# Layer 1's value columns multiplied from centred rows between the steps of a rank search, FFN's part added later over 256 inner rows; the gate norm's weights multiplied on GpSimd

## Chip, cores and metric

One core of a Trainium2 chip runs one program. The metric is the device time of one execution in microseconds (us). Before the change the median of 3 runs is 1879.77 us.

## What is computed

Two layers over 625 graph nodes with 1024 features. The part that matters here is the end of layer 0 and the start of layer 1, cut from the reference:

```python
x = x + gnn(xn, ...) * gate(...) + mix(xn)             # layer 0's graph and attention parts
# layer 0's FFN
h = _layernorm(x, ln_g, ln_b)
h = _qlinear(h, w1)          # int8 rows times ternary weights; 1024 -> 256
h = gelu(h)
x = x + _qlinear(h, w2)      # the same, 256 -> 1024
# layer 1
xn = _layernorm(x)
... xn @ W for W of 4096 columns: graph W, Wq, Wk, Wv
def _quant_act_int8(x):
    amax = jnp.quantile(jnp.abs(x), 1.0 - 0.005)
```

The quantile needs one number out of all 625 x 1024 (later 625 x 256) absolute values: the rank search finds it in steps, each of which counts the values over some thresholds and then narrows them.

## The kernel before

The nodes stand as T = 5 row tiles of P = 125. A dense product of 625 x 1024 rows with 512 columns is a "group": eight chunks of weights (128 inner rows by 512 columns) by five tiles, each in three matmuls (`three`: high by high, low by high, high by low part), 120 matmuls. One stream of chunks feeds all groups. SP loads a chunk into one of 4 stages (`w_stage`), ScalarE or GpSimd makes the high part (`w_hi`; `split_act`, or the first half of `split_chunk`), GpSimd or VectorE the low part (`w_lo`; `split_low`, `split_dve`), and 8 slots hold them. A slot is free again (`w_used`) when the last row tile of a group has used its chunk. A turned group (`dense_turned`) computes its product transposed, with 24 shorter matmuls a chunk.

All engines' queues are written out by hand in program order; nothing reorders them but what semaphores hold back. The order of the stretch in question:

1. Layer 0's gate: `proj_second` feeds the transposed rows (PE transposes, ScalarE copies `xt_hi`, VectorE subtracts `xt_lo`); then two gate groups, the first in two passes (rows 0 to 2, rows 3 and 4), the second row by row (`dense_pe_rows`).
2. Beside the second group, row by row on VectorE: `gate_evac` (z = nat * ps, x1 = x1 + z), `norm_var`, `candidates` (the largest 8 of each 256 absolute values), `norm_rows` (a Newton step for the root, then (x1 - mean) * lng, then * root + lnb into `nat`).
3. `find_rank` over those candidates: five rounds of seven thresholds (`pick_pe`, `sum_dve`), then three finer steps. VectorE and TensorE take turns. Then the rows are quantised (`round_part`, `clip_part`), multiplied by `w1q`, GELU, and `find_rank` again over 256 columns.
4. `down_pe`/`down_add` add the FFN into x1 tile by tile; `down_var`, `again_scale`, `again_norm`, `tile_turn`, `tile_high`, `tile_low` normalise and transpose each tile.
5. Layer 1's eight groups in the order `L1_ORDER = (6, 2, 4, 3, 5, 7, 0, 1)`; 6 is the first half of the value columns, 2 to 5 are turned. The first group is done tile by tile, between the transposes of step 4:

```python
for m in range(T):
    PE.wait_ge(S("x_low_a"), m + 1)
    PE.wait_ge(S("down_free"), 6 if m < 2 else 2 * T)
    dense_part(c0, g0, (m,), beside_again(m))
```

From the second group on GpSimd splits each chunk, high and low part.

## Time and profile before

| | |
|---|---|
| median of 3 runs | 1879.77 us (1879.57 to 1880.76) |
| profiled execution, first to last instruction | 1878.8 us |
| TensorE busy | 1794.9 us (96%) |
| VectorE busy | 1023.3 us (54%) |
| ScalarE busy | 478.5 us (25%) |
| GpSimd busy | 701.1 us (37%) |
| mean granted TensorE clock | 0.979 |

The profiled execution's own time is its span, 1878.8 us, and what lies around it; the runs shown have a median 1.0 us above that span. A busy TensorE is one with a matmul under way; the granted clock is 1.0 at 2.4 GHz and 0.5 at 1.2 GHz. A wait is given in brackets behind a row, with the engine and the tile that ended it.

### The profile page before, as it was taken

The numbers are of one execution on the slowest core, as the hardware profiler recorded it, in microseconds if no ns is written. First come the engines' busy times: TensorE is split into PE (matmuls) and PEld (weight loads), VectorE is DVE, ScalarE is ACT, GpSimd is POOL, SyncE is SP. The second block draws the span as 40 slices with busy tenths as digits, with TensorE's granted clock in tenths as the row PEclk, the third lists the DMA queues.
The fourth block names the chain that finished last, engine by engine and source line by source line (L and its number), as shares of the span: only waits on it lengthen the run. The fifth ranks groups of instructions, "written<-read, shape, count | busy, mean of one in ns | idle before, by whom it ended". The sixth has DMA issues, their size and how long they took to land.

```text
span 1878.8 us, 28666 instructions
## 1 busy us (share of the span) xinstructions
PE 1794.9 (96%) x9953; PEld 1477.4 (79%) x9953; DVE 1023.3 (54%) x2540; ACT 478.5 (25%) x1055; POOL 701.1 (37%) x609
## 2 busy tenths in 40 slices
PE   6999999999999999999999999954999999999999
PEld 4876689987777778787777887742899888878987
DVE  7888999997254543526354356786632224362311
ACT  3139956662010110101011145243100000111100
POOL 2110000003634435353534444200485552345862
PEclk9999999999999999999999999956999999999999
DMA  4532222224213121231313534110354351113322
GB/s 134 154 109 77 73 86 79 75 67 129 91 38 89 45 72 56 66 86 47 94 33 113 172 84 131 45 46 7 96 164 146 104 156 51 37 55 118 90 73 66
DMA packets 129282, 162.23 MB, mean 86 GB/s; under 512 B 14288, under 2 KB 75368, under 8 KB 128922
## 3 DMA queue, kind: packets, MB, share of 16 engines
q1 hardware_dynamic: 100848, 120.93, 21.5%
q10 hardware_dynamic: 22250, 23.53, 4.0%
q0 software_dynamic: 6080, 16.40, 2.9%
q8 instruction: 63, 1.03, 0.2%
q14 instruction: 41, 0.34, 0.1%
HBM read 135.51 MB, written 25.30 MB: 86 GB/s over the span
## 4 chain that ended last, share of the span: by engine, by line
PE 84%; DVE 6%; ACT 6%; issue 1%; DVEq 1%; DMA 1%; POOL 0%; ACTq 0%; SPq 0%
PE ps L367 22%; PE ps L368 22%; PE ps L369 21%; PE ps L1236 9%; PE ps L892 3%; ACT sc_col L838 2%; ACT sc_row L837 1%; PE ps L1201 1%; DVE w_lo L318 1%; PE ps L881 1%; PE ps L1156 1%; DMA nat<-in_x 1%; ACT w_hi L313 1%; PE ps L1183 1%; PE ps L1211 0%
## 5 line engine op out<-in xcount | busy, mean ns | idle before, releaser
L367 PE MATMUL ps<-w_hi,xt_hi 128*125 128x512 f32 x1320 | 539.0, 408 | 9.1 <-DVE xt_lo L549 3.5
L256 POOL TENSOR_TENSOR w_hi<-w_stage,zero 128x512 fp32r<-128x512 f32 x256 | 276.8, 1081 | 684.4 <-PE ps L369 670.0
L368 PE MATMUL ps<-w_lo,xt_hi 128*125 128x512 f32 x1320 | 523.0, 396 | 0.0
L369 PE MATMUL ps<-w_hi,xt_lo 128*125 128x512 f32 x1320 | 521.5, 395 | 0.0
L259 POOL TENSOR_TENSOR w_lo<-w_stage,w_hi 128x512 fp32r<-128x512 f32 x256 | 346.2, 1352 | 20.1
L367 PEld LDWEIGHTS ps<-w_hi,xt_hi 128*125 128x125 f32 x1320 | 246.6, 187 | 67.1 <-DVE xt_lo L549 4.3
L369 PEld LDWEIGHTS ps<-w_hi,xt_lo 128*125 128x125 f32 x1320 | 246.0, 186 | 63.3
L368 PEld LDWEIGHTS ps<-w_lo,xt_hi 128*125 128x125 f32 x1320 | 246.3, 187 | 53.5
L367 PE MATMUL ps<-xt_hi,w_hi 128*128 128x314 f32 x736 | 250.5, 340 | 1.3 <-DVE ring L2430 0.6
L369 PE MATMUL ps<-xt_hi,w_lo 128*128 128x314 f32 x736 | 225.9, 307 | 0.0
L368 PE MATMUL ps<-xt_lo,w_hi 128*128 128x314 f32 x736 | 225.7, 307 | 0.0
L367 PEld LDWEIGHTS ps<-xt_hi,w_hi 128*128 128x128 f32 x736 | 139.0, 189 | 6.8 <-POOL w_lo L259 1.1
L368 PEld LDWEIGHTS ps<-xt_lo,w_hi 128*128 128x128 f32 x736 | 139.5, 190 | 2.7
L369 PEld LDWEIGHTS ps<-xt_hi,w_lo 128*128 128x128 f32 x736 | 139.0, 189 | 0.0
L1420 DVE TENSOR_TENSOR nat<-nat,ps 125x512 f32<-125x512 f32 x80 | 53.9, 687 | 120.6 <-PE ps L369 120.2
L1286 ACT ACTIVATE xt_hi<-mtmp 128x313 fp32r<-128x313 f32 (+1 forms) x128 | 59.5, 465 | 194.1 <-DVEq L1390 194.1
L1236 PE MATMUL ps<-a_hi,xn_hi 125*128 125x313 f16 (+1 forms) x640 | 106.4, 297 | 1.7 <-DVE mtmp L1386 1.6
L1236 PE MATMUL ps<-a_hi,xn_lo 125*128 125x313 f16 (+1 forms) x640 | 106.3, 296 | 0.0
L313 ACT ACTIVATE w_hi<-w_stage 128x512 fp32r<-128x512 f32 x118 | 73.0, 629 | 108.1 <-PE ps L369 62.4
L856 DVE TENSOR_SCALAR hot_col<-iota,slot 128x626 f16<-128x626 f16 x240 | 91.6, 382 | 0.1
L292 POOL DMA_DIRECT2D pre<-ring x30 | 16.2, 540 | 194.7 <-DVE ring L476 192.8
L1236 PEld LDWEIGHTS ps<-a_hi,xn_hi 125*128 125x128 f16 x640 | 61.5, 97 | 26.9 <-issue 2.4
...
## 6 DMA issues: line engine op xcount, KB each, us to landing
...
```

The costliest lines, as they stand in the source:

```text
L256: POOL.tensor_tensor(w_hi[:, q, :], w_stage[:, q % NST, :], zero[:].to_broadcast([128, 512]), ALU.add).then_inc(S("hi_done"), 1)
L259: POOL.tensor_tensor(w_lo[:, q, :], w_stage[:, q % NST, :], w_hi[:, q, :].bitcast(F32), ALU.subtract).then_inc(S("split_done"), 1)
L313: ALE.activation(w_hi[:, c % NSL, :], w_stage[:, c % NST, :], ACT.Copy).then_inc(S("hi_done"), 1)
L367: PE.matmul(dst, l_hi, r_hi, start=first, stop=False)
L368: PE.matmul(dst, l_hi, r_lo, start=False, stop=False)
L369: return PE.matmul(dst, l_lo, r_hi, start=False, stop=last)
L838: ALE.activation(sc_col[j][:], sc_lo[j][:], ACT.Copy, scale=e_col1[:, bass.ds(c, 1)]).then_inc(S("sc_scaled"), 1)
L856: DVE.tensor_scalar(hot_col[q][:], iota1_16[:], slot[:, 0, bass.ds(c, 1)], None, ALU.is_equal)
L892: PE.matmul(group_banks(gm)[0], hot_row[q][:, 0:P], hot_col[q][:, 0:C1], start=(j == 0), stop=(j == 1), skip_group_check=True)
L1236: return PE.matmul(dst, x16[:, t, k * 128:(k + 1) * 128], a16[:, t, h0:h0 + hn], start=first, stop=last)
L1286: ALE.activation(xt_hi[:, j // 2, h0:h0 + hn], mtmp[j % 4][:, 0:hn], ACT.Copy).then_inc(S("mt_hi"), 1)
L1420: DVE.tensor_tensor(u_, u_, ps[0:P, m, :], ALU.add).then_inc(S("bank_free"), 1)
```

## The change

- Layer 1's group of value columns 6 comes second in `L1_ORDER`, and is computed in two parts. With c the gate's result less its row mean, the normalised row is (c + f - mean of f) * root, f being the FFN's output. c @ W is computed beforehand: 120 matmuls from `xc_hi`, `xc_lo`, the transposed centred rows, stored to DRAM in `p_part`. f's part goes over its 256 inner rows: `w2k` is the ternary second FFN weight less its mean over the columns, w2k @ W is 32 matmuls stored in `m_part`, and `late_pe` later multiplies the quantised inner rows with that in 20 matmuls; `evac_late` adds `p_late` and the bias.
- These 152 matmuls (`part_pe`) are given out by `in_gap(n)`, n at a time, between the steps of the rank searches, in the first FFN product and in the norm that follows. Their eight chunks are a group of their own (`C_GAP`).
- `w2k` is made on VectorE (the mean) and ScalarE (the subtraction), transposed by 16 transposes on TensorE in the gate's second pass, and copied by ScalarE.
- Rows 0 to 3 of the gate norm: ScalarE subtracts the mean (`centre`), GpSimd multiplies with `lng` (`times_gain`); VectorE's Newton step and last multiplication for row m stand after row m+1's gate work. The centred rows stay in x1; ScalarE adds the mean back after the norm of step 4.
- GpSimd also makes the low parts of the `C_GAP` chunks, subtracts `xc_lo` (`low_x`), and splits all eight chunks of layer 1's first group.
- The first dense group of layer 1 is a turned one, and starts when all five tiles are done.

The diff, cut to its core:

```diff
+    C_REL, C_PROJ, C_GATE, C_GAP, C_L1, D_L1 = 80, 208, 224, 240, 248, 240
+    L1_ORDER = (2, 6, 4, 3, 5, 7, 0, 1)
+    TURNED1 = (0, 2, 3, 4)
+    LATE = 1
...
+    def turn_w2(i):
+
+        PE.wait_ge(S("w2_centred"), 2)
+        if i == 3:
+            PE.wait_ge(S("w2_copied"), 1)
+        for k in (2 * i, 2 * i + 1):
+            for j in range(FFN0 // 128):
+                o = (k % 2) * FFN0 + j * 128
+                t_ = PE.transpose(ps[:, W2_BANKS[i], o:o + 128], w2k[:, j, k * 128:(k + 1) * 128], ident[:])
+        t_.then_inc(S("w2_turned"), 1)
...
+    def beside_gate(k):
+        if k in (3, 4, 5, 7):
+            turn_w2((3, 4, 5, 7).index(k))
...
+    def low_x(m):
+
+        POOL.wait_ge(S("x_hi"), T + m + 1)
+        POOL.tensor_tensor(xc_lo[:, m].rearrange("p k n -> p (k n)"), xc_raw[:, m].rearrange("p k n -> p (k n)"),
+                           xc_hi[m][:].rearrange("p k n -> p (k n)").bitcast(F32), ALU.subtract).then_inc(S("x_low"), 1)
+
...
+    def part_pe():
+
+        PE.wait_ge(S("bank_free"), (g1 + 2) * T + 4)
...
+        for m in range(T):
+            PE.wait_ge(S("x_low"), T + m + 1)
+            PE.wait_ge(S("part_out"), m + 1)
+            dst = ps[0:P, PART_BANKS[m % 2], :]
+            for k in range(KT):
+                PE.matmul(dst, xc_hi[m][:, k, :], w_hi[:, k, :], start=(k == 0), stop=False)
+                yield
+                PE.matmul(dst, xc_hi[m][:, k, :], w_lo[:, k, :], start=False, stop=False)
+                yield
+                t_ = PE.matmul(dst, xc_lo[:, m, k, :], w_hi[:, k, :], start=False, stop=(k == KT - 1))
+                if m == T - 1:
+                    t_.then_inc(S("w_used"), 1)
+                elif k == KT - 1:
+                    t_.then_inc(S("part_full"), 1)
+                if k == KT - 1:
+                    part_out(2 + m, p_part[m], P)
+                yield
...
+    for c in range(C_GATE + KT, C_GATE + KT + 2):
+        split_act(c)
+    for j in range(FFN0 // 128):
+        ALE.wait_ge(S("w2_room"), 1)
+        ALE.activation(w2k[:, j, :], w2q[:, j, :], ACT.Identity, bias=w2_mean[:, j:j + 1]).then_inc(S("w2_centred"), 1)
+    for i in range(4):
+        copy_w2(i)
+    for c in range(C_GATE + KT + 2, C_GAP):
         split_act(c)
...
+        if k == 5:
+            DVE.wait_ge(S("wq_done"), 2)
+            DVE.tensor_reduce(w2_mean[:], w2q[:], AX.X, ALU.add)
+            DVE.drain()
+            DVE.tensor_scalar(w2_mean[:], w2_mean[:], -1.0 / D, None, ALU.mult).then_inc(S("w2_room"), 1)
...
+    def times_gain(m):
+
+        POOL.wait_ge(S("x_norm"), T + m + 1)
+        POOL.tensor_tensor(nat[:, m, :], x1[:, m, :], lng[:], ALU.mult).then_inc(S("h_gain"), 1)
...
+            DVE.drain()
+            DVE.wait_ge(S("h_gain"), m + 1)
             DVE.scalar_tensor_tensor(o, o, r, lnb[:], ALU.mult, ALU.add).then_inc(S("h_norm"), 1)
 
     rk_up = small("rk_up", [P, 4, 7], F16)
...
         gate_evac(1, m)
         norm_var(m)
+        square_act(m)
+        if m < T - 1:
+            centre(m)
         if m >= 1:
-            candidates(habs, "h_abs", D, m - 1)
-        norm_rows(m)
-        square_act(m)
-        if m == T - 1:
-            copy_h(0)
-            copy_h(1)
-        absolute(nat, habs, "h_abs", D, m)
+            norm_root(m - 1)
+            norm_out(m - 1)
+            absolute(nat, habs, "h_abs", D, m - 1)
+        if m >= 2:
+            candidates(habs, "h_abs", D, m - 2)
+        for c in {2: (0, 1), 3: (2, 3, 4), 4: (5, 6, 7)}.get(m, ()):
...
+    for m in range(3):
+        times_gain(m)
+    for c in range(3):
+        split_low(C_GAP + c, c)
+    times_gain(3)
+    for c in range(3, KT):
+        split_low(C_GAP + c, c)
+    for m in range(T):
+        low_x(m)
+
+    turn_x(0)
+    turn_h(0)
+    in_gap(32)
+    turn_x(1)
+    copy_x(1)
+
+    done["chunks"] += 5 * KT
...
@@ -1723,15 +1882,14 @@
                     t_ = PE.matmul(ps[0:n_, 0, j:j + 1], hot[:, j, o:o + n_], ones_b[0:P, :], start=(o == 0), stop=(o == 128),
                                    skip_group_check=True)
             t_.then_inc(S("rk_part"), 1)
+            in_gap(2)
             PE.wait_ge(S("rk_copied"), i + 1)
             PE.matmul(ps[:, 1, 0:columns], ones16[:], q_part7[:, 0:columns], start=True, stop=True).then_inc(S("rk_count"), 1)
...
+    def turn_rest(i):
+
+        if i in (0, 2, 4):
+            turn_h(1 + i // 2)
+            copy_h(1 + i // 2)
+        elif i < ROUNDS + 1:
+            turn_x(2 + i // 2)
+            copy_x(2 + i // 2)
...
+    in_gap(8)
+    down_pe(0)
+    in_gap(8)
...
+    DVE.tensor_scalar(h_mean[:], h_neg[:], -1.0, None, ALU.mult)
+    mk = sig(DVE.drain(), "dve_step")
+    DVE.wait_ge(S("w_used"), NSL + C_GAP + KT)
+    DVE.tensor_copy(gq_whole[:], gq_t[:]).then_inc(S("gq_whole"), 1)
+    wait(ALE, mk)
+    for m in range(T):
+        mk_mean = sig(ALE.activation(x1[:, m, :], x1[:, m, :], ACT.Identity, bias=h_mean[:, m:m + 1]), "act_step")
+
+    for c in range(C_L1, C_L1 + NSL):
+        split_chunk(c, c % NSL, c // NST + 1)
...
+    in_gap(6)
+    for m in range(1, T):
+        if m + 2 < T:
+            down_pe(m + 2)
+        tile_turn(m, AGAIN)
+        in_gap(12)
+    in_gap(8 * KT * T)
+    PE.wait_ge(S("x_low"), AGAIN + T)
+    PE.wait_ge(S("part_out"), 2 + T)
+
+    def late_pe(g):
+
+        PE.wait_ge(S("gq_whole"), 1)
+        for m in range(T):
+            PE.wait_ge(S("bank_free"), (g + g0) * T + (3, 3, 4, 5, 5)[m])
+            for k in range(FFN0 // 128):
+                if m == 0:
+                    PE.wait_ge(S("split_done"), NST + c0 + g * KT + k + 1)
...
+                if m == T - 1:
+                    last.then_inc(S("w_used"), 1 if k == 0 else KT - 1)
+                elif k == FFN0 // 128 - 1:
+                    last.then_inc(S("bank_full"), 1)
+
```

The first place where the order of a queue differs: ScalarE (ACT), from the last of the gate's fed chunks to the splitting of the second gate group's eight chunks (`w_hi<-w_stage`; the first of the rows shown is the first group's last). Before:

```order
L313 ACTIVATE w_hi<-w_stage 128x512 [waits w_used,landed3]
L313 ACTIVATE w_hi<-w_stage 128x512 [waits w_used,landed0]
L313 ACTIVATE w_hi<-w_stage 128x512 [waits w_used,landed1]
L313 ACTIVATE w_hi<-w_stage 128x512 [waits w_used,landed2]
L313 ACTIVATE w_hi<-w_stage 128x512 [waits w_used,landed3]
```

Now:

```order
L312 ACTIVATE w_hi<-w_stage 128x512 [waits w_used,landed3]
L312 ACTIVATE w_hi<-w_stage 128x512 [waits w_used,landed0]
L312 ACTIVATE w_hi<-w_stage 128x512 [waits w_used,landed1]
L1619 ACTIVATE w2k<-w2q,w_mean 128x1024 [waits w2_room] x2
L1478 ACTIVATE w2k_t<-ps 128x512 [waits w2_turned,w2_room]
L1478 ACTIVATE w2k_t<-ps 128x512 [waits w2_turned] x3
L312 ACTIVATE w_hi<-w_stage 128x512 [waits w_used,landed2]
L312 ACTIVATE w_hi<-w_stage 128x512 [waits w_used,landed3]
```

Six of the second gate group's eight chunks now stand behind the four copies of `w2k_t`, the last of which waits for transposes that TensorE does after chunk 7 of the first gate group's second pass.

The second place: GpSimd (POOL), from the low parts of the projection and gate chunks (x24) on. Before it waits there for VectorE's low parts, and then runs its loop over layer 1's chunks:

```order
L276 TENSOR_TENSOR w_lo<-w_stage,w_hi 128x512 [waits hi_done] x24
L264 UNCONDITIONAL_BRANCH [waits split_done]
L264 ISA
L255 ISA [waits landed0]
L256 TENSOR_TENSOR w_hi<-w_stage,zero 128x512 [waits w_used]
```

Now:

```order
L279 TENSOR_TENSOR w_lo<-w_stage,w_hi 128x512 [waits hi_done] x24
L1762 TENSOR_TENSOR nat<-x_8789,lng 125x1024 [waits x_norm] x3
L279 TENSOR_TENSOR w_lo<-w_stage,w_hi 128x512 [waits hi_done] x3
L1762 TENSOR_TENSOR nat<-x_8789,lng 125x1024 [waits x_norm]
L279 TENSOR_TENSOR w_lo<-w_stage,w_hi 128x512 [waits hi_done] x5
L1544 TENSOR_TENSOR xc_lo<-xc_raw,xc_hi_12097 128x1000 [waits x_hi]
L1544 TENSOR_TENSOR xc_lo<-xc_raw,xc_hi_12098 128x1000 [waits x_hi]
L1544 TENSOR_TENSOR xc_lo<-xc_raw,xc_hi_12099 128x1000 [waits x_hi]
L1544 TENSOR_TENSOR xc_lo<-xc_raw,xc_hi_12100 128x1000 [waits x_hi]
L1544 TENSOR_TENSOR xc_lo<-xc_raw,xc_hi_12101 128x1000 [waits x_hi]
L259 TENSOR_TENSOR w_hi<-w_stage,zero 128x512 [waits w_used,landed0]
L262 TENSOR_TENSOR w_lo<-w_stage,w_hi 128x512 [waits hi_done]
```

GpSimd's 17 operations between the gate and layer 1 are new, and so is its splitting of the first group's chunks; the fourth multiplication with `lng` stands behind three low parts.

The third place: ScalarE at the end of the norm of step 4 (`xt_hi` of the last tile is the last that it does for it). Before:

```order
L2094 ACTIVATE xt_hi<-ps 128x4x125 [waits x_turn]
L2262 DMA bias_o<-in_bias 125x1024
L2264 DMA a_bd<-in_pm 64x64
L2265 DMA a_bd<-in_pm 64x64
L2383 DMA pre<-ring 125x512 [waits bank_free] x5
```

Now:

```order
L2261 ACTIVATE xt_hi<-ps 128x4x125 [waits x_turn]
L2466 ACTIVATE x_8789<-x_8789,h_mean 125x1024 [waits dve_step]
L2466 ACTIVATE x_8789<-x_8789,h_mean 125x1024 x4
L2482 DMA bias_o<-in_bias 125x1024
L2484 DMA a_bd<-in_pm 64x64
L2485 DMA a_bd<-in_pm 64x64
L1555 ACTIVATE part<-ps 125x512 [waits part_st0,w_used]
L1557 DMA p_part<-part 125x512 [waits part_out]
```

The copy that empties the last bank of the part products (`part<-ps`) stands behind five additions of the mean and three DMAs; TensorE's first matmul of the first dense group of layer 1 waits for it:

```order
L366 MATMUL ps<-xt_hi,w_hi 128x314 [waits split_done,bank_free,part_out,x_low]
```

## Rows read from the trace of the kernel before

**Rows 1.** The page: the chain that ended last, shares of the span by engine.

```profile
PE 84%; DVE 6%; ACT 6%; issue 1%; DVEq 1%; DMA 1%; POOL 0%; ACTq 0%; SPq 0%
```

**Rows 2.** Windows: length, busy PE, PEld, DVE, ACT, POOL (xinstructions), PEclk, DMA, GB/s.

```profile
1236.00:1240.00 4.00, 3.14 (x22) 2.87 (x23) 3.74 (x19) 3.02 (x6) 0.00 (x0) 0.50 0.06 23
...
1308.00:1312.00 4.00, 3.11 (x8) 2.43 (x9) 3.53 (x8) 1.52 (x2) 0.00 (x0) 0.50 0.00 0
```

**Rows 3.** Groups, TensorE, 1166.4 to 1222.5: the gate's matmuls, high by high.

```profile
L367 PE MATMUL ps<-w_hi,xt_hi 128*125 128x512 f32 x80 | 31.6, 395 | 1.8 <-DVE xt_lo L1169 1.8
```

**Rows 4.** Timeline of the gate's feed: start, duration, engine, operation, [idle before].

```profile
1160.30 0.68 DVE L1168 TENSOR_TENSOR xt_lo<-ps,xt_hi 128x500 fp32r<-128x500 f32 x1 [1.01 <-ACT xt_hi L1163]
...
1161.38 0.70 PE L1156 MATMUL ps<-ident,nat 125*128 125x125 f32 x5
...
1166.47 0.50 PE L367 MATMUL ps<-w_hi,xt_hi 128*125 128x512 f32 x1 [1.75 <-DVE xt_lo L1169]
```

**Rows 5.** Timeline, VectorE: two reductions of different length in the rank search.

```profile
1257.18 0.28 DVE L1823 TENSOR_REDUCE q_cnt<-q_hot 125x31 f16<-125x124 f32 x1
...
1259.77 0.42 DVE L1823 TENSOR_REDUCE q_cnt<-q_hot 125x63 f16<-125x252 f32 x1
```

**Rows 6.** Timeline: four low parts on GpSimd, and VectorE beside them.

```profile
1191.13 5.78 POOL L276 TENSOR_TENSOR w_lo<-w_stage,w_hi 128x512 fp32r<-128x512 f32 x4
...
1194.56 1.20 DVE L1580 SCALAR_TENSOR_TENSOR x<-x,z 125x512 f32<-125x512 f32 x1
```

**Rows 7.** Timeline, VectorE (ScalarE in the first), gate rows 1 to 4.

```profile
1208.49 1.15 ACT L1627 ACTIVATE habs<-x,h_neg 125x1024 f32<-125x1024 f32 x1 [0.50 <-DVEq L1621]
...
1213.59 0.68 DVE L1572 TENSOR_TENSOR z<-nat,ps 125x512 f32<-125x512 f32 x1
1214.30 0.69 DVE L1580 SCALAR_TENSOR_TENSOR x<-x,z 125x512 f32<-125x512 f32 x1
...
1215.40 1.41 DVE L1599 MAX8 cand<-habs 125x8 f32<-125x256 f32 x4
...
1217.89 1.28 DVE L1645 SCALAR_TENSOR_TENSOR nat<-x,h_neg,lng 125x1024 f32<-125x1024 f32 x1
...
1227.30 0.68 DVE L1572 TENSOR_TENSOR z<-nat,ps 125x512 f32<-125x512 f32 x1
...
1234.41 1.41 DVE L1599 MAX8 cand<-habs 125x8 f32<-125x256 f32 x4
```

**Rows 8.** Timeline of the last norm: a step beside GpSimd's splitting, and without it.

```profile
1661.44 1.49 POOL L256 TENSOR_TENSOR w_hi<-w_stage,zero 128x512 fp32r<-128x512 f32 x1
1663.01 1.28 POOL L259 TENSOR_TENSOR w_lo<-w_stage,w_hi 128x512 fp32r<-128x512 f32 x1
...
1662.18 0.77 DVE L532 SCALAR_TENSOR_TENSOR t<-rs,va 125x1 f32<-125x1 f32 x1
...
1685.99 0.22 DVE L532 SCALAR_TENSOR_TENSOR t<-rs,va 125x1 f32<-125x1 f32 x1
```

**Rows 9.** Timeline, VectorE: the seven thresholds of a round of the rank search.

```profile
1246.61 1.29 DVE L1762 TENSOR_SCALAR r_hot<-r_hi,q_took 125x160 bf16<-125x160 int16 x7
```

**Rows 10.** Timeline, the norm before layer 1, and the start of its first two groups.

```profile
1297.28 1.40 DVE L2040 SCALAR_TENSOR_TENSOR x<-ps,qrs,x 125x512 f32<-125x512 f32 x2
...
1308.15 1.26 DVE L2101 TENSOR_TENSOR xt_lo<-ps,xt_hi 128x500 fp32r<-128x500 f32 x2
1308.89 0.79 PE L367 MATMUL ps<-w_hi,xt_hi 128*125 128x512 f32 x1 [3.44 <-DVE xt_lo L2101]
...
1313.85 0.16 DVE L530 RECIPROCAL rs<-t 125x1 f32<-125x1 f32 x1 [1.01 <-ACT t L2082]
...
1315.13 1.26 DVE L2101 TENSOR_TENSOR xt_lo<-ps,xt_hi 128x500 fp32r<-128x500 f32 x2
...
1334.14 0.60 ACTq L2265 DMA_DIRECT2D a_bd<-in_pm  x1
...
1343.59 0.38 PE L367 MATMUL ps<-xt_hi,w_hi 128*128 128x314 f32 x1 [0.65 <-DVE ring L2430]
```

More of the change, by code:

```diff
@@ new lines, in part_out @@
+    def part_out(n, dst, rows):
+        if n < 1 + T:
+            ALE.wait_ge(S("part_full"), n + 1)
+        else:
+            ALE.wait_ge(S("w_used"), NSL + C_GAP + KT)
+        if n >= 2:
+            ALE.wait_ge(S(f"part_st{n % 2}"), 16 * (n // 2))
+        ALE.activation(part[0:rows, n % 2, :], ps[0:rows, PART_BANKS[n % 2], :], ACT.Copy).then_inc(S("part_out"), 1)
+        ALE.wait_ge(S("part_out"), n + 1)
+        ALE.dma_start(dst, part[0:rows, n % 2, :]).then_inc(S(f"part_st{n % 2}"), 16)
@@ L1490, in build, with in_gap @@
+    steps_left = part_pe()
+    def in_gap(n):
+        for _ in itertools.islice(steps_left, n):
+            pass
     MAGIC = 1.5 * 2.0 ** 23
@@ L1644, in norm_rows, with norm_out @@
         DVE.tensor_tensor(r, r, t, ALU.mult)
-        DVE.scalar_tensor_tensor(o, x1[:, m, :], h_neg[:, m:m + 1], lng[:], ALU.add, ALU.mult)
-        DVE.drain()
+    def norm_out(m):
+        r, o = rs[:, m:m + 1], nat[:, m, :]
         if m == T - 1:
+            DVE.scalar_tensor_tensor(o, x1[:, m, :], h_neg[:, m:m + 1], lng[:], ALU.add, ALU.mult)
+            DVE.drain()
             c = slice(0, 512)
@@ L2127, in build @@
     clip_part(gq_t[:, :, (T - 1) * P:NODES], KT + T)
-    for m in range(4):
+    in_gap(8)
+    down_pe(0)
+    in_gap(8)
+    for m in range(1, 3):
         down_pe(m)
```

389 lines of the change are left out of this document (238 added, 151 removed).

## The prediction

> **What bounds the kernel now.** The chain of waits puts 84% of the span on TensorE, 6% each on VectorE and ScalarE [rows 1], so only stretches where TensorE waits can give or cost much. I read the windows and the groups next, to find those, then the timelines of each. There are three. In the gate TensorE needs 240 matmuls (80 of each kind) for the 56 us of the view [rows 3]: 0.233 us each, 5.6 for a row tile's 24. VectorE needs more in the second group: its work on a row begins every 6.86 us (1213.59 for row 2, 1227.30 for row 4) [rows 7]. In the rank searches the two take turns; the granted clock is 0.50 [rows 2]. In the norm before layer 1 VectorE's cadence is 1315.13 - 1308.15 = 7.0 us a tile, of which 1.0 is a wait for ScalarE [rows 10], against 5.6 of matmuls. So the group of value columns, 28 us on TensorE, already lies almost wholly under VectorE's norm. Moving it away frees little there; what VectorE, ScalarE and GpSimd do in its place decides. That is the main point of this forecast.
>
> **The change part by part.** The profiled execution lasted 1878.8 us, 1.0 under the median of the runs; I sum against 1878.8. Times after T0 count from `down_add(0)`, 1297.28 [rows 10].
>
> (a) The mean of `w2k` in the feed: reducing 252 elements takes 0.14 us more than 124 [rows 5], so 2048 cost 2.2 us on VectorE. Its steps there wait 1.0 for ScalarE each [rows 4], which hides about one. Ends 0 and 2.2; I take **+1.0**.
>
> (b) Sixteen transposes in the gate's second pass, 0.14 each (5 in 0.70) [rows 4], 2.2 in all, with a stop of 0.1 for ScalarE's subtraction: **+2.3**. Nothing hides them, TensorE is busy in that pass.
>
> (c) The queue of the second gate group's chunks. ScalarE splits two, then subtracts the mean, then copies four banks, the last transposed behind chunk 7 of the pass; only then come chunks 2 to 7 (the first place shown). GpSimd's low parts take 5.78/4 = 1.45 each [rows 6]. So the group's first chunk finds its operands about 2.8 us after the pass's end and the last at 10.0; TensorE finishes row 0 10.7 us after the pass instead of 5.6: **+5.1**. Before, all eight were split ahead.
>
> (d) The gate rows. Before: row 0's work begins 4 x 6.86 before 1227.30, at 1199.9, and the last `candidates` end at 1235.8: 35.9 us [rows 7]. With the multiplication by `lng` (1.28) [rows 7] gone from rows 0 to 3, VectorE needs about 5.6 and keeps pace with TensorE: row 4 starts 22.3 after row 0. But its tail is longer: the 8.5 us of before (1227.30 to 1235.8), and now also row 3's last multiplication (1.3), two more `candidates` (1.4 each), and a wait of 2.4 for GpSimd's `times_gain(3)`, which stands behind three low parts; 0.3 of it overlaps: 14.7. That makes 37.0, +1.1.
>
> To this comes what GpSimd does to VectorE. In the last norm one and the same step of the root takes 0.77 beside GpSimd's splitting and 0.22 without it; the 0.77 end at 1662.95, which is where GpSimd's operation ends (1661.44 + 1.49) [rows 8]. In the gate x1 = x1 + z took 1.20 beside low parts, 0.69 without [rows 6, 7]. So the two shut each other out for a whole operation when VectorE reads two operands from SBUF. The new GpSimd operations are four multiplications of 1024 columns (2 x 1.28 [rows 8] = 2.6 us) and eight low parts of 1.45; VectorE's `gate_evac`, variance, root and last multiplication meet them. Laid out row by row (each `times_gain` starts 4.5 after a row's work begins), rows 1 to 3 run late by 0.6, 1.5 and 1.3, row 4 begins at 26.7, the wait for `times_gain(3)` ends at 31.8, row 3 is out at 35.0, row 4's root at 39.8 after two stops, its norm ends at 44.0 and the last `candidates` at 46.9. That is 9.9 more than 37.0. Ends 0 and 12 x 1.45 = 17; I take 9.9, **+11.0** with the above.
>
> The Trainium skill says the same of the ports (page SBUF — State Buffer, section "Who interferes with whom"): VectorE's second pair is shared with GpSimd, and whoever comes first holds it for the whole instruction. It adds that copies and `tensor_scalar` can take both pairs. By the page's rule the thresholds of the rank search would be shut out too; no row of this case has one beside GpSimd.
>
> (e) The first search. `in_gap(2)` fits into the 1.29 us of thresholds [rows 9]; the 32 matmuls ahead, the 5 in each finer step and TensorE's extra transposes of centred rows leave +0.8, after VectorE's own low parts (off its queue now) are taken off. GpSimd's five `low_x` of 2.6 stand beside it; a block costs at most 2.6 less the 1.0 that VectorE waits anyway, so 0 to 8.0 in all. VectorE's operations are about half of the two-operand kind: 4.2, together **+5.0**.
>
> (f) The up product and second search: matmuls in the gaps keep the clock up, which was 0.50 [rows 2]: **-0.7**. Ends -3 and +3.
>
> (g) The norm. VectorE's chain shortens to 6.1 a tile (the wait of 1.0 goes, since no dense matmuls hold the transposes) [rows 10], so the last low part would end at T0 + 31.3. But GpSimd splits layer 1's first eight chunks there, 1.49 and 1.28 [rows 8], in place of ScalarE and VectorE earlier; the blocks cost 0 to 12, and I take 7.7 by the 0.55 of rows 8 on some 14 steps: T0 + 39.0. Then ScalarE: the last `part<-ps` copy stands behind five additions of the mean (1.15 each [rows 7]) and three DMA issues (0.60 each [rows 10]), and TensorE waits for it (the third place shown). 5.8 + 1.8 + 0.6 = 8.1. The turned group starts at T0 + 47.2, where it started at 1343.59, T0 + 46.3 [rows 10]. It runs its first us at the low clock, as the first group did (8 matmuls in 3.11 us, 0.39 each [rows 2]): 1.5. Later `late_pe`, 20 x 0.233 = 4.7, and 2.2 of waiting, because GpSimd can split group 3's first chunks only when `late_pe` has freed slots. **+9.3**.
>
> Sum: 1.0 + 2.3 + 5.1 + 11.0 + 5.0 - 0.7 + 9.3 = +33.0; 1911.8 in the span, **1912.8** as a median.
>
> **The rivals.**
>
> R1, no blocking: the few long cases of rows 6 and 8 are not typical, and new operations fall between VectorE's. Then 9.9 + 4.2 + 7.7 = 21.8 go: 1891.0. For it: nearly all VectorE steps beside GpSimd in the trace are short enough to slip in. Against it: the match to the hundredth in rows 8. 0.19.
>
> R2, ScalarE's tail is hidden (another wait ends later, or the mean is added beside VectorE's last tile): -8.1, 1904.7. Against: the addition waits for a drain behind the last low part. 0.10.
>
> R3, other side: GpSimd is quick enough never to be waited for. That is 21.8, the 2.4 of `times_gain(3)`, the 5.1 of (c) and the 2.2 of (g), 31.5: 1881.3, not slower than before. It decides from about 0.7 us for 512 columns, which is VectorE's time for them [rows 7]. The rows show GpSimd at 1.28 to 1.49. 0.11, since all ends of (e) and (f) may add to it.
>
> R4, the clock stays at 0.50 through both searches, as it does now [rows 2]: some 60 matmuls in the first at 0.39 instead of 0.23, 8 us of it exposed, and 3 in the second: 1923.8. 0.08.
>
> R5, the thresholds are shut out too: (e) costs 0.8 + 8.0, +3.8, 1916.6. It is the port rule of the page named in (d). Nothing in the trace speaks for or against it. 0.05.
>
> That the change does not do what it says: 128 of the 152 matmuls stand ahead of the norm in program order, the rest in it. If chunks or `xc_lo` come late, TensorE stops in a gap, and that is in (e) and R4.
>
> **How the numbers follow.** The forecast has 0.47, R1 0.19, R2 0.10, R3 0.11, R4 0.08, R5 0.05. Some 0.2% (3.8 us) is what a measurement of this kernel can tell from no change. Not slower needs at most 1883.5: R3 mostly, with R1's lower edge (its (f) at -3). R3 I split 0.04 faster, 0.05 same, 0.02 slower, and give 0.02 of R1 to the two. So faster 0.05, same 0.06, slower 0.89. The range reaches from under R1 (1887, its (a) and (f) low) to 1923, which leaves out most of R3, half of R4 and the ends of (d) and (g), 0.18 in all. All of the forecast's own case lies in 1904 to 1921.
>
> **What the profile of after would show.** (b, c) A wait of TensorE of 2 to 3 us for `split_done` at the second gate group, and `w_hi` of its chunks 2 to 7 behind `w2k_t`. (d) From row 0's `gate_evac` to the last `candidates` some 47 us, 2.6 us for `nat` on GpSimd, VectorE steps of 0.2 that take 1 to 2, and VectorE's idle time ended by POOL in row 4. (e) Thresholds still 1.29, a search of 30 us rather than 26. (g) The last `xt_lo` 39 us after `down_add(0)`, the turned group 8 later, its wait ended by ACT `part`. The prediction is wrong if VectorE's steps keep their times beside GpSimd (R1), if TensorE's wait ahead of the turned group ends with `xt_lo` (R2), or if the feed or the searches wait for operands that I have as ready. A gain would need GpSimd's rows near 0.7.

## The result and the profile after

The changed kernel takes 1917.71 us (median of 4 runs, 1916.51 to 1919.33), beside 1880.26 for the one before on the same chip: a ratio of 1.0201, 95% interval 1.0189 to 1.0214. It is 37.5 us slower; whether that is more or less than 2% the interval leaves open. The forecast was 1912.8 with a range of 1887 to 1923: the result lies inside, 4.9 us above the forecast. The profiled execution spans 1915.2 us, 36.4 more than before; the sum of the prediction was 33.0.

To see where the 36.4 arise I divided both traces at six instructions, each a row of VectorE's or TensorE's timeline: the first `z<-nat,ps` of gate row 0, the copy `r_hi<-cand` that begins the first search, the first `h_t<-h_t,qs` behind it, `down_add(0)` (the first `x<-ps,qrs,x`, T0), the first matmul of the first turned group, and the last turned evacuation `ring_t<-ps,bias_t`.

| stage (us) | before | after | difference | forecast |
|---|---|---|---|---|
| start to row 0 (a, b, c) | 1200.1 | 1207.1 | +7.0 | +8.4 |
| gate rows (d) | 35.9 | 45.1 | +9.2 | +11.0 |
| first search (e) | 26.2 | 35.5 | +9.3 | +5.0 |
| up product, second search (f) | 35.1 | 37.4 | +2.3 | -0.7 |
| T0 to the first turned group (g) | 46.3 | 44.4 | -1.9 | +0.9 |
| from there to the last turned evacuation (g) | 125.2 | 135.8 | +10.5 | +8.4 |

The six differences make 36.4: behind the last of these points both kernels need 410.0 us.

The dividing points of the changed kernel in VectorE's timeline, and the steps read below (start, duration, operation, [idle before]); the rows of before at the same places are [rows 7, 10]:

```profile
1207.09 0.69 DVE L1692 TENSOR_TENSOR z<-nat,ps 125x512 f32<-125x512 f32 x1 [8.37 <-PE ps L368]
...
1231.40 0.67 DVE L1692 TENSOR_TENSOR z<-nat,ps 125x512 f32<-125x512 f32 x1
1232.10 1.68 DVE L1700 SCALAR_TENSOR_TENSOR x<-x,z 125x512 f32<-125x512 f32 x1
...
1234.48 1.56 DVE L1771 SCALAR_TENSOR_TENSOR t<-rs,va 125x1 f32<-125x1 f32 x1
...
1246.57 2.81 DVE L1786 SCALAR_TENSOR_TENSOR nat<-nat,rs,lnb 125x512 f32<-125x512 f32 x1
...
1252.14 0.24 DVE L1914 COPY r_hi<-cand 125x160 int16<-125x160 int16 x1
...
1256.23 2.16 DVE L1940 SCALAR_TENSOR_TENSOR q_took<-q_cand,q_took 128x1 f32<-128x1 f32 x1
...
1287.68 1.00 DVE L2153 TENSOR_SCALAR h_t<-h_t,qs 128x625 f32<-128x625 f32 x2
...
1325.05 1.40 DVE L2207 SCALAR_TENSOR_TENSOR x<-ps,qrs,x 125x512 f32<-125x512 f32 x2
```

Beside them GpSimd, in the changed kernel's timeline:

```profile
1233.19 2.84 POOL L1762 TENSOR_TENSOR nat<-x,lng 125x1024 f32<-125x1024 f32 x1
1235.98 2.53 POOL L279 TENSOR_TENSOR w_lo<-w_stage,w_hi 128x512 fp32r<-128x512 f32 x2
...
1246.06 2.77 POOL L1544 TENSOR_TENSOR xc_lo<-xc_raw,xc_hi 128x1000 fp32r<-128x1000 f32 x1
1256.07 2.30 POOL L1544 TENSOR_TENSOR xc_lo<-xc_raw,xc_hi 128x1000 fp32r<-128x1000 f32 x1 [7.24 <-ACT xc_raw L1538]
```

Three steps of VectorE end with an operation of GpSimd or right behind it. The step on one element that begins at 1234.48 ends at 1236.04, GpSimd's multiplication with `lng` at 1236.03. The addition of `lnb` that begins at 1246.57 has some 0.7 us of work and takes 2.81: GpSimd's subtraction holds it till 1248.83, and it ends 0.55 later. `q_took` from 1256.23 ends at 1258.39, `xc_lo` at 1258.37. That is the pattern of [rows 8], at the places forecast under (d) and (e).

TensorE in one round of the first search (4.46 us from one count to the next), and two windows of the same stretch (columns as in [rows 2]). First the timeline:

```profile
1263.23 1.73 PE L1882 MATMUL ps<-ones_b,r_hot 125*128 125x1 bf16 x14
1264.88 0.79 PE L1579 MATMUL ps<-w_lo,xc_hi 128*125 128x512 f32 x1
1265.47 0.63 PE L1581 MATMUL ps<-w_hi,xc_lo 128*125 128x512 f32 x1
1265.90 0.23 PE L1887 MATMUL ps<-q_part,ones 128*128 128x7 f16 x1
1265.99 1.91 PE L1528 MATMUL ps<-ident,x 125*128 125x125 f32 x8
1267.69 1.73 PE L1882 MATMUL ps<-ones_b,r_hot 125*128 125x1 bf16 x14
```

And the windows:

```profile
1252.00:1260.00 8.00, 6.81 (x44) 5.44 (x44) 5.56 (x23) 6.03 (x13) 2.30 (x1) 0.61 0.17 66
1260.00:1268.00 8.00, 8.00 (x44) 6.31 (x43) 4.01 (x22) 1.24 (x4) 2.31 (x1) 0.50 0.01 2
```

In the second window TensorE is busy for 8.00 of 8 us and the granted clock is 0.50, its lower level. VectorE is busy for half of it. In this search TensorE no longer takes turns with VectorE, it sets the length of the rounds. The prediction did not have that.

The gate's feed, the last step of it. Before, TensorE's five transposes stand together and it waits once, 1.75 us (TensorE's timeline of the kernel before, and [rows 4]):

```profile
1164.02 0.70 PE L1156 MATMUL ps<-ident,nat 125*128 125x125 f32 x5
```

In the changed kernel it waits twice, since VectorE is making the mean of `w2k`; and the last step of that, on two elements, starts beside a low part of GpSimd and ends with it, at 1164.00 and 1163.98:

```profile
1162.64 0.59 PE L1155 MATMUL ps<-ident,nat 125*128 125x125 f32 x4
1162.71 1.27 POOL L279 TENSOR_TENSOR w_lo<-w_stage,w_hi 128x512 fp32r<-128x512 f32 x1 [1.02 <-ACT w_hi L312]
1162.80 1.20 DVE L1674 TENSOR_SCALAR w_mean<-w_mean 128x2 f32<-128x2 f32 x1
1164.83 0.33 PE L1155 MATMUL ps<-ident,nat 125*128 125x125 f32 x1 [1.59 <-DVE xt_lo L1168]
1166.90 0.50 PE L366 MATMUL ps<-w_hi,xt_hi 128*125 128x512 f32 x1 [1.75 <-DVE xt_lo L1168]
```

The wait at the second gate group and the two ends of (g), from TensorE's timeline of the changed kernel:

```profile
1199.89 0.50 PE L366 MATMUL ps<-w_hi,xt_hi 128*125 128x512 f32 x1 [1.44 <-POOL w_lo L279]
...
1201.13 0.50 PE L366 MATMUL ps<-w_hi,xt_hi 128*125 128x512 f32 x1 [0.28 <-POOL w_lo L279]
...
1369.40 0.60 PE L366 MATMUL ps<-xt_hi,w_hi 128*128 128x314 f32 x1 [7.36 <-issue]
...
1406.24 0.41 PE L366 MATMUL ps<-xt_hi,w_hi 128*128 128x314 f32 x1 [2.38 <-POOL w_lo L262]
```

TensorE's last matmul ahead of 1369.40 are transposes that end at 1362.0. What it waits for is not named there ("issue"); VectorE's and ScalarE's rows show it:

```profile
1362.70 0.68 DVE L2268 TENSOR_TENSOR xt_lo<-ps,xt_hi 128x500 fp32r<-128x500 f32 x1 [0.15 <-ACT xt_hi L2261]
...
1364.57 4.25 ACT L2466 ACTIVATE x<-x,h_mean 125x1024 f32<-125x1024 f32 x4
1368.73 0.57 ACT L1555 ACTIVATE part<-ps 125x512 f32<-125x512 f32 x1
```

The last low part is done at 1363.38, T0 + 38.3 (forecast 39.0); `part` at 1369.30, and TensorE starts 0.1 us later.

### The profile page after: what moved, and what is told of

It is laid out like the page before. It is cut to its first block, busy times and chain, and to the rows that moved or that the text cites. A ratio compares the mean times of both kernels' runs of the same rounds, so it can differ in the third digit from the quotient of the medians.

```text
span 1915.2 us, 28990 instructions
## 1 busy us (share of the span) xinstructions
PE 1831.9 (96%) x10061; PEld 1499.7 (78%) x10061; DVE 1040.4 (54%) x2539; ACT 507.9 (27%) x1098; POOL 741.3 (39%) x630
## 4 chain that ended last, share of the span: by engine, by line
PE 85%; DVE 6%; ACT 5%; issue 2%; DVEq 1%; DMA 1%; POOL 1%; ACTq 0%; SPq 0%; POOLq 0%
PE ps L366 22%; PE ps L367 21%; PE ps L368 21%; PE ps L1235 9%; PE ps L891 3%; ACT sc_col L837 2%; ACT sc_row L836 1%; PE ps L1200 1%; DVE w_lo L317 1%; PE ps L880 1%; PE ps L1155 1%; DMA nat<-in_x 1%; PE ps L1182 1%; ACT w_hi L312 1%; PE ps L1210 0%
## 5 line engine op out<-in xcount | busy, mean ns | idle before, releaser
L366 PE MATMUL ps<-w_hi,xt_hi 128*125 128x512 f32 x1280 | 522.8, 408 | 8.5 <-DVE xt_lo L548 3.5
L367 PE MATMUL ps<-w_lo,xt_hi 128*125 128x512 f32 x1280 | 506.6, 396 | 0.0
L368 PE MATMUL ps<-w_hi,xt_lo 128*125 128x512 f32 x1280 | 505.3, 395 | 0.0
L262 POOL TENSOR_TENSOR w_lo<-w_stage,w_hi 128x512 fp32r<-128x512 f32 x258 | 349.6, 1355 | 20.2
L366 PEld LDWEIGHTS ps<-w_hi,xt_hi 128*125 128x125 f32 x1280 | 238.8, 187 | 66.2 <-POOL w_lo L279 5.5
L368 PEld LDWEIGHTS ps<-w_hi,xt_lo 128*125 128x125 f32 x1280 | 238.2, 186 | 61.3
L367 PEld LDWEIGHTS ps<-w_lo,xt_hi 128*125 128x125 f32 x1280 | 238.6, 186 | 51.5
L279 POOL TENSOR_TENSOR w_lo<-w_stage,w_hi 128x512 fp32r<-128x512 f32 x40 | 58.3, 1476 | 64.9 <-ACT w_hi L312 64.8
```

The costliest lines, as they stand in the source:

```text
L262: POOL.tensor_tensor(w_lo[:, q, :], w_stage[:, q % NST, :], w_hi[:, q, :].bitcast(F32), ALU.subtract).then_inc(S("split_done"), 1)
L279: POOL.tensor_tensor(w_lo[:, q, :], w_stage[:, q % NST, :], w_hi[:, q, :].bitcast(F32), ALU.subtract).then_inc(S("split_done"), 1)
L366: PE.matmul(dst, l_hi, r_hi, start=first, stop=False)
L367: PE.matmul(dst, l_hi, r_lo, start=False, stop=False)
L368: return PE.matmul(dst, l_lo, r_hi, start=False, stop=last)
```

## The experiments

Twelve kernels, all edits of the changed one. They ran on three chips, each beside the kernel before, whose median on these chips is 1880.0 to 1880.5. e1, e6, e7, e9 and e11 leave work out; the others keep all of it. "Less" and "more" below are against the changed kernel's 1917.71. The stages are cut as above.

| run | median | row 0 | gate | search | f | to turned | rest |
|---|---|---|---|---|---|---|---|
| after | 1917.71 | 1207.1 | 45.1 | 35.5 | 37.4 | 44.4 | 135.8 |
| e1_no_low_x | 1913.36 | 1207.2 | 43.0 | 34.1 | 37.3 | 44.3 | 135.8 |
| e2_rounds | 1920.59 | 1210.6 | 45.1 | 33.5 | 39.5 | 47.1 | 135.2 |
| e3_tail | 1911.93 | 1209.3 | 45.0 | 35.4 | 35.9 | 39.2 | 135.6 |
| e4_queue | 1913.37 | 1203.2 | 45.0 | 35.4 | 36.0 | 43.9 | 135.7 |
| e5_gain_dve | 1916.50 | 1208.2 | 45.3 | 35.4 | 37.6 | 44.5 | 136.0 |
| e6_no_gpsimd_low | 1908.46 | 1211.1 | 36.8 | 32.7 | 36.1 | 45.3 | 135.2 |
| e7_no_norm_split | 1909.99 | 1210.6 | 45.1 | 35.4 | 36.0 | 37.9 | 135.3 |
| e8_all | 1909.41 | 1206.2 | 45.0 | 33.5 | 38.7 | 41.2 | 135.8 |
| e9_no_turn_x | 1921.46 | 1210.5 | 45.0 | 37.3 | 37.3 | 44.3 | 135.8 |
| e10_tail_queue | 1907.50 | 1203.7 | 45.0 | 35.3 | 36.9 | 39.2 | 135.7 |
| e11_floor | 1890.52 | 1203.8 | 36.8 | 33.5 | 37.0 | 31.9 | 135.9 |
| e12_dve_low | 1906.29 | 1205.9 | 42.3 | 35.8 | 35.9 | 39.2 | 135.6 |

Two columns move without an edit to them, from one execution to the next. Row 0 comes up to 4 us later, partly because all that stands ahead of the gate's feed ends sooner or later, partly by the granted clock in the feed (the last section), and (f) lies between 35.9 and 37.6. So the stage that was edited decides what an edit did. A difference of two medians contains the rest too.

**e1_no_low_x.** GpSimd's five subtractions go.

```diff
-            t_ = ALE.activation(xc_raw[:, m, 4 * j:4 * j + 4, :], view, ACT.Copy)
+            t_ = ALE.activation(xc_lo[:, m, 4 * j:4 * j + 4, :], view, ACT.Copy)
-        POOL.tensor_tensor(xc_lo[:, m]..., xc_raw[:, m]..., xc_hi[m]..., ALU.subtract).then_inc(S("x_low"), 1)
+        POOL.sem_inc(S("x_low"), 1)
```

> The five subtractions that make xc_lo on GpSimd are left out (ScalarE's second copy writes the unsplit values into xc_lo, so the low parts are not low parts). Theory A, shutting out: in the changed kernel one-element steps of the rank search took 2.16, 0.48 and 1.41 us instead of 0.16 beside these subtractions, 3.6 us together, and the last gate row's additions of lnb took 1.60 and 2.81 instead of about 0.7, part of it beside the first of them. So the time falls by 4 to 6 us, and the steps go back to 0.16. Theory B, the first search is long because TensorE has more to do in each round (two matmuls ahead of the sum, eight transposes behind it): it falls by less than 1 us, and rounds of 4.1 us stay.

4.4 us less as a median, 3.5 in the stages: 2.1 in the gate, 1.4 in the search. A is right that they hold VectorE. But the search loses 1.4 where the held steps sum to 3.6, and the rounds keep 4.47 us: TensorE's own work covers the rest. B is right about the rounds that stay, and wrong about the sum.

**e2_rounds.** The two matmuls leave the rounds.

```diff
-            in_gap(2)
...
     down_pe(0)
-    in_gap(8)
+    in_gap(20)
```

> The two part matmuls in each of six rounds of the first search are moved behind the first product of the second FFN weight. Theory B: VectorE's wait between the cast of the counts and their comparison goes from 1.01 back to 0.28 us, 0.73 times 6 rounds = 4.4 us; the 12 matmuls cost about 1.4 where they go, so the time falls by 3. Theory A (only the shutting out makes the first search long): no change, or 1 us more.

The sign is wrong, 2.9 us more. The search does lose 2.0. But (f) grows by 2.1 and the norm by 2.7, and both stages can be read. VectorE's timeline of this run, behind `down_add(0)`:

```profile
1328.69 1.40 DVE L2206 SCALAR_TENSOR_TENSOR x<-ps,qrs,x 125x512 f32<-125x512 f32 x2
...
1333.10 1.41 DVE L2206 SCALAR_TENSOR_TENSOR x<-ps,qrs,x 125x512 f32<-125x512 f32 x2 [1.11 <-PE ps L2197]
```

`down_add(1)` waits for TensorE's second product, which stands behind 20 matmuls instead of 8. It starts 4.4 us behind the first, where it was 3.4 in the changed kernel (1325.05 and 1328.46). In (f) VectorE waits 6.40 us for GELU's first value instead of 4.10. ScalarE's timeline of this run shows why:

```profile
1300.69 0.60 ACT L1555 ACTIVATE part<-ps 125x512 f32<-125x512 f32 x1 [4.78 <-PE ps L1581]
...
1301.65 0.47 ACT L2181 ACTIVATE gl<-ps,qrs 125x256 f32<-125x256 f32 x1 [0.37 <-ACT part L1555]
```

With 12 part matmuls fewer ahead, the last matmul of a row tile of the part products now falls behind the up product, and the copy of that tile stands ahead of GELU in ScalarE's queue. GELU waits for a matmul that it does not need. In the changed kernel this copy is made ahead of the up product (1284.92), and in e8, which has the same move, it stands ahead of GELU again and waits 3.77 us. Moved out of a busy stage, the work became exposed in two others.

**e3_tail.** ScalarE's five additions and three DMAs move behind `in_gap(8 * KT * T)`.

```diff
-    wait(ALE, mk)
-    for m in range(T):
-        mk_mean = sig(ALE.activation(x1[:, m, :], ..., bias=h_mean[:, m:m + 1]), "act_step")
...
     in_gap(8 * KT * T)
+    wait(ALE, mk)
+    for m in range(T):
+        mk_mean = sig(ALE.activation(x1[:, m, :], ..., bias=h_mean[:, m:m + 1]), "act_step")
```

> ScalarE's five additions of the mean and its three DMAs move behind the last copy of the part products. Theory: TensorE waits for that copy alone, so the first turned group starts right behind the last xt_lo (1363.4 in the changed kernel, where it started at 1369.4): the time falls by 5.5 us. Rival: something else is as late (VectorE's work on c_nat till 1368.9, GpSimd's splitting, the late group's data), and it falls by less than 2.

5.8 us less, as expected, 5.2 of it in the stage of the edit. TensorE now starts behind the last low part (timeline of this run):

```profile
1364.18 0.68 DVE L2268 TENSOR_TENSOR xt_lo<-ps,xt_hi 128x500 fp32r<-128x500 f32 x1 [0.15 <-ACT xt_hi L2261]
...
1364.91 0.63 PE L366 MATMUL ps<-xt_hi,w_hi 128*128 128x314 f32 x1 [1.39 <-DVE xt_lo L2268]
```

**e4_queue.** Splits and copies take turns on ScalarE.

```diff
-    for i in range(4):
-        copy_w2(i)
-    for c in range(C_GATE + KT + 2, C_GAP):
-        split_act(c)
+    split_act(C_GATE + KT + 2)
+    for c, i in ((3, 0), (4, 1), (5, 2), (6, None), (7, 3)):
+        if i is not None:
+            copy_w2(i)
+        split_act(C_GATE + KT + c)
```

> ScalarE splits the second gate group's chunks 2 to 7 between the copies of w2k_t instead of behind them. Theory: TensorE's waits for w_lo at that group (1.44 + 5 x 0.28 us) go, row 0 is ready 4 us sooner, and the time falls by 3 to 4.4 us. Rival: GpSimd's low parts then stand beside VectorE's additions of the first gate group and the loads are late anyway; it falls by less than 1.5.

4.3 us less. From the first matmul behind the feed (1167.50) to row 0 it is 35.7 us, in the changed kernel 40.2 (1166.90 to 1207.09): 4.5, both with a granted clock of 1.00 in the feed. The same stretch is 37.2 (e10, e11) against 41.7 (e3, e5, e6) where the clock was 0.83, and 38.1 (e8, e12) against 42.5 to 42.8 (e2, e7, e9) at 0.66: again 4.5 each. Term (c) was right.

**e5_gain_dve.** The multiplication with `lng` goes back to VectorE, in `norm_out`.

```diff
-            DVE.wait_ge(S("h_gain"), m + 1)
+            DVE.wait_ge(S("x_norm"), T + m + 1)
+            DVE.tensor_tensor(o, x1[:, m, :], lng[:], ALU.mult)
+            DVE.drain()
```

> The multiplication with lng of gate rows 0 to 3 goes back from GpSimd to VectorE. Theory A, shutting out: VectorE has 1.28 us more a row but is no longer held by 2.4 us on GpSimd in each, and nobody waits for them; the gate from row 0's first addition to the last candidates (44.9 us in the changed kernel) gets 0 to 3 us shorter, and the time falls by 0 to 3. Rival: VectorE bounds these rows, and four times 1.28 are added: 4 to 5 us more.

1.2 us less, and the gate keeps its 45 us (45.3). Four operations on the other engine gave nothing: what they took off VectorE they gave back in waits and held steps.

**e6_no_gpsimd_low.** As e1, and the low parts of eight chunks go.

```diff
-        split_low(C_GAP + c, c)
+        POOL.wait_ge(S("hi_done"), C_GAP + c + 1)
+        POOL.sem_inc(S("split_done"), 1)
```

> GpSimd makes neither xc_lo (as in the run without these subtractions) nor the low parts of the part products' eight chunks; stale low parts are used. Theory A: beside the 4 to 6 us of that run, the last gate rows lose the steps that stood beside low parts (1.68, 1.56, 0.93, 2.24, 2.38, 1.60, 2.81 us where 0.69, 0.22, 0.16, 1.28, 1.28, 0.7, 0.7 are usual, together some 8 us), so the gate is 37 to 39 us instead of 44.9 and the time falls by 10 to 13 us. Rival: the tail of the gate is long because more VectorE work stands in it; 5 to 7 us less.

9.3 us less as a median; in the profiled execution row 0 was 4 us late for no reason of the edit, and the two stages give 11.2, as theory A has it. The gate goes to 36.8, 8.3 shorter, and the search 2.9. The multiplications with `lng` are still GpSimd's here, and the fourth still holds a step of the root: 1.57 us (1236.49) instead of 0.22. The two additions of `lnb` of row 4, in VectorE's timeline of this run, are 0.75 each again (1.60 and 2.81 in the changed kernel):

```profile
1243.70 0.75 DVE L1783 SCALAR_TENSOR_TENSOR nat<-nat,rs,lnb 125x512 f32<-125x512 f32 x1
1244.37 0.75 DVE L1785 SCALAR_TENSOR_TENSOR nat<-nat,rs,lnb 125x512 f32<-125x512 f32 x1
```

**e7_no_norm_split.** GpSimd leaves layer 1's first eight chunks unsplit.

```diff
     for c in range(C_L1, C_L1 + NSL):
-        split_chunk(c, c % NSL, c // NST + 1)
+        POOL.wait_ge(S(f"landed{c % NST}"), 16 * (c // NST + 1))
+        POOL.wait_ge(S("w_used"), c + 1)
+        POOL.sem_inc(S("hi_done"), 1)
+        POOL.sem_inc(S("split_done"), 1)
```

> GpSimd does not split the eight chunks of layer 1's first group; stale parts are used. Theory A: the steps of the root that took 0.4 to 1.26 us instead of 0.16 or 0.22 beside the splitting sum to 6.5 us, so the last xt_lo comes 6 us sooner behind down_add(0) (38.3 us in the changed kernel) and the time falls by 5 to 6.5. Rival: ScalarE and TensorE set the norm's cadence as they did before the change; it falls by less than 2.

7.7 us less, 6.4 of it in the stage of the norm. The last steps of the root are short again in this run:

```profile
1343.71 0.16 DVE L535 TENSOR_TENSOR rs<-rs,t 125x1 f32<-125x1 f32 x1
1343.95 0.16 DVE L2219 SCALAR_TENSOR_TENSOR m_first<-mv,rs 125x1 f32<-125x1 f32 x1
```

The same two in the changed kernel, beside the splitting:

```profile
1344.73 1.03 DVE L535 TENSOR_TENSOR rs<-rs,t 125x1 f32<-125x1 f32 x1
1345.85 0.92 DVE L2219 SCALAR_TENSOR_TENSOR m_first<-mv,rs 125x1 f32<-125x1 f32 x1
```

**e8_all.** The edits of e2, e3 and e4 together.

> The three moves together: part matmuls out of the first search's rounds, the mean and DMAs behind the last copy, chunk splits between the copies of w2k_t. By their own expectations 3 + 5.5 + 4 = 12.5 us less than the changed kernel, some 1905, still slower than before the change, since the shutting out stays. Rival: they overlap, and less than 9 come.

8.3 us less, not 12.5: the first edit costs. The rival's number came, for another reason than overlap.

**e9_no_turn_x.** TensorE has 24 transposes less in the search.

```diff
+        if m >= 2:
+            PE.sem_inc(S("x_turn"), 1)
+            return
         for k in range(KT):
             t_ = PE.transpose(ps[:, X_BANKS[k // 4], ...], x1[:, m, ...], ident[0:P, 0:P])
```

> TensorE's eight transposes of the centred rows 2, 3 and 4 are left out (the copies behind them take old contents of the banks). Theory B2: in the changed kernel TensorE is busy without a gap through the rounds of the first search and sets their length, at the low clock: 14 matmuls of the counts (1.7 us), two part matmuls (1.2) and eight transposes (1.7) make 4.47 us, where the rounds of before took 3.28. So three rounds get up to 1.2 us shorter, the search goes from 35.5 us to some 32.5 and the time falls by 2.5 to 3.5. Rival: the steps held by GpSimd set the rounds; less than 1 us.

Neither theory has the sign: 3.7 us more as a median. The profiled execution is 5.0 longer, 1.8 of it in the search and 3.4 up to row 0, where nothing was edited. With the transposes gone, ScalarE's copies and so `low_x` come sooner, and now stand beside the thresholds. VectorE's timeline of this run:

```profile
1260.50 1.26 DVE L1943 SCALAR_TENSOR_TENSOR q_took<-q_cand,q_took 128x1 f32<-128x1 f32 x1
1261.84 3.35 DVE L1923 TENSOR_SCALAR r_hot<-r_hi,q_took 125x160 bf16<-125x160 int16 x7
```

And GpSimd's:

```profile
1262.32 2.29 POOL L1547 TENSOR_TENSOR xc_lo<-xc_raw,xc_hi 128x1000 fp32r<-128x1000 f32 x1 [0.58 <-ACT xc_raw L1541]
```

Seven thresholds that took 1.29 [rows 9] take 3.35: 2.06 more, about the length of the operation beside them, and once more in a later round (3.37). So the thresholds are shut out too, the mechanism of R5. In the changed kernel they kept 1.29, because `q_took`, held ahead of them, had already waited GpSimd's operation out. About TensorE theory B2 is borne out all the same: from one round's thresholds to the next the two rounds without transposes take 5.66 and 5.62 us, less the hold 3.6 and 3.5, against 4.46 with them. The page of R5's rule, SBUF — State Buffer of the Trainium skill, section "Who interferes with whom", has this case, and this trace agrees with it. It also says that a VectorE instruction with at most one input in SBUF is not in the way, unless it runs in one of the modes that use both ports. Here the trace agrees again: `x<-ps,qrs,x`, which reads one tile from PSUM and one from SBUF (`qrs` is a single column), takes 1.41 beside GpSimd's splitting (1342.13) and 1.40 without (1325.05).

**e10_tail_queue.** e3 and e4.

> The mean and DMAs behind the last copy, and chunk splits between the copies of w2k_t, without the move out of the rounds. They stand in different stages, and alone they gave 5.8 and 4.3 us: 10 less than the changed kernel, some 1907.6. Rival: they overlap and give less than 8.

1907.50. The two add up; that they do so to a tenth of a microsecond is luck, as the runs of one kernel are 1 to 5 us apart. This version keeps all of the work.

**e11_floor.** e10, with what e1, e6 and e7 leave out.

> The two moves of the run before, and GpSimd's low parts of the part products' chunks, its xc_lo and its splitting of layer 1's first group left out: what the plan costs with GpSimd's operations away and both queues in order. If the parts add up: 1917.7 - 10.1 - 9.3 - 7.7 = 1890.6, still 10 us over the kernel before, which then is TensorE's and ScalarE's work of the plan itself (transposes, the rounds at the low clock, the late 20 matmuls). Rival: the loss is GpSimd's and the queues' alone, and the time is at or under 1880.

1890.52, as the parts add up. So the operations left out cost 17.0 us (1907.50 to 1890.52) at the places that the change gave them. They cost it chiefly by held steps: in none of these kernels does a wait of VectorE between 1205 and 1400 end with GpSimd. GpSimd's four multiplications with `lng` are still in. With them the plan is 10 us over the kernel before: the search 7.3 longer, (f) 1.9, the late group's stage 10.7, row 0 3.7, the gate 0.9, against 14.4 gained from T0 to the first turned group (31.9 instead of 46.3). That last is the most that moving the group away can give, since here nobody splits the first group's chunks.

**e12_dve_low.** e10, with those low parts and `xc_lo` on VectorE.

```diff
-        POOL.wait_ge(S("x_hi"), T + m + 1)
-        POOL.tensor_tensor(xc_lo[:, m]...
+        DVE.wait_ge(S("x_hi"), T + m + 1)
+        DVE.tensor_tensor(xc_lo[:, m]...
...
+        for c in {3: (0, 1), 4: (2, 3, 4)}.get(m, ()):
+            split_dve(C_GAP + c)
...
+            if i % 2 == 0:
+                low_x(1 + i // 2)
```

> The two moves, and the low parts of the part products' chunks and xc_lo are made by VectorE instead of GpSimd (nothing is left out). Theory A: VectorE needs 0.68 us a chunk, 5.4 in the gate's last rows against the 8.3 that GpSimd's cost there, and its five subtractions (1.3 each) lie in rounds that TensorE sets; so 3 to 5 us less than the run with the two moves alone, some 1903 to 1905. Rival: VectorE's own work in the rounds is exposed, and it is no faster.

1.2 us less than e10, not 3 to 5 (2.2 by the two edited stages; row 0 came 2.2 later in this execution). The gate gets 2.7 shorter; the search 0.5 longer, since the first `low_x` in it waits 2.8 us for ScalarE's copies and the last stands alone behind the last step. No version beat the kernel before.

## Why the prediction came out as it did

The mechanisms of (a) to (d) and of (g) were right; (e) and (f) failed. By steps:

- **(a)** 1.8 instead of 1.0. From the last transposes of the feed to the matmul behind them it is 4.26 us (1162.64 to 1166.90), before 2.45 (1164.02 to 1166.47), and 4.26 to 4.29 in all thirteen profiled executions with this feed. The sum over 2048 elements took 2.28, forecast 2.2; the step behind it was held 1.0 by GpSimd, which the term had not. That this hardly shows in the 7.0 to row 0 is chance: the changed kernel reached these transposes 1.4 us sooner than the kernel before, others of the thirteen up to 1.1 later.
- **(b)** 2.0 instead of 2.3, from that matmul to row 0: 35.7 us in e4, where (c) is gone, before 33.6 (1166.47 to 1200.11).
- **(c)** 4.5 instead of 5.1; e4 gives it back. GpSimd's low parts came every 1.24 us (the waits at 1199.89 and 1201.13), not every 1.45.
- **(d)** 9.2 instead of 11.0. Row 4 begins 24.3 us after row 0 instead of 26.7, since in rows 1 and 2 VectorE still waits 2.8 and 1.2 us for TensorE and the holds fall into that; the tail behind it is 20.7, forecast 20.2. GpSimd's part is 8.3 (e6) and what the multiplications with `lng` add, which e6 keeps, forecast 9.9. The wait of 2.4 for `times_gain(3)` never shows as a wait: it ends inside the step that is held from 1234.48 to 1236.04. So the forecast sign "VectorE's idle time ended by POOL in row 4" did not appear. The price 2.6 for `times_gain` was 2.40 to 2.84.
- **(g)** 8.6 instead of 9.3, with errors that cancel: the norm's held steps 6.4 (e7) instead of 7.7; ScalarE's tail 6.0 instead of 8.1, because its five additions ran in 5.3 and the three DMAs were issued beside them, not behind; and the late stage 10.5 instead of 8.4. Of these 10.5 TensorE's 20 matmuls are 4.7 (group L2581 and L2582, 10 each, 0.233 apart), the wait behind them 2.4 (1406.24), the start at the low clock about 2.2 (the first block took 9.1 us where the next three took 6.9 to 7.0 each); some 1.2 I have not traced.

R1, no blocking, is dead: the held steps show the blocking, and e11 beside e10 prices it at 17.0 (without the multiplications with `lng`), forecast 21.8. R2 was wrong as a forecast and right as a remedy: e3. R3 had no chance: GpSimd took 1.04 to 1.6 us for 512 columns. R5's mechanism is in the changed kernel at least once, in (a): the held step there reads one tile. On the thresholds it did not act there, as forecast, but it does in e9.

**The step that failed is (e)**, 9.3 us instead of 5.0. It says that "`in_gap(2)` fits into the 1.29 us of thresholds". The two matmuls do not stand beside the thresholds but between the counts and their sum, where VectorE waits: 1.01 us (ahead of L1938) instead of 0.28 (ahead of L1780, where nothing else of VectorE's fills it). Behind the sum come eight transposes in every round, where before a single round had them, and the 0.8 left for all that was far too little. TensorE, which waited in these rounds before, became their bound at 4.47 us against 3.28, at the low clock; e6 has rounds of 4.45 to 4.47 with nothing of GpSimd's in them, e9 rounds of 3.6 without the transposes, and e2 gains 2.0 by the two matmuls. GpSimd's share was sized 4.2 and measured 1.8 (e11 beside e10) to 2.9 (e6), so e's error sits in TensorE's part: about 7.3, since e11 has the search at 33.5 against 26.2 with nothing of GpSimd's left in it. Part of this is R4, which I gave 0.08: the clock stayed at 0.50 through most of the rounds (0.61 from 1252 to 1260). How the 7.3 divide between the matmuls, the transposes and the clock no run separates.

**(f)** failed in sign, 2.3 instead of -0.7, and not by the clock. From the first `h_t<-h_t,qs` to GELU's first candidates it is 11.2 us (1287.68 to 1298.85), before 9.1; from there to T0 26.2, before 26.0. In the second of these stretches, the second search, the granted clock did rise, from 0.57 to 0.87 (0.80 to 1.00 in the experiments), and the search took 25.7 us at its best: at most 0.3 come back. The loss is in the up product, for which the term had nothing: seven part matmuls stand between its own, of which this is one, and then GELU begins 8.3 us after the product's first matmul (1289.57 to 1297.83), before 6.0 (1264.29 to 1270.31).

```profile
1290.52 0.78 PE L1579 MATMUL ps<-w_lo,xc_hi 128*125 128x512 f32 x1
```

So the result is nearer to the forecast than its terms are. (b), (c), (d) and (g) were sized 3.4 us too high together, (a), (e) and (f) 8.1 too low, and the 1.4 by which this execution was ahead at the feed covers part of the difference. In the profiled execution 3.4 us remain, and that it is no more is luck.

What is open: how (f) and the row 0 column fall out in the timed executions, of which one in each kernel has a trace, and so about 2 us of each median.
